# Doubled edge steps with the first scatter in front, an expert table by partition, and empty rows from two queues

## The reference, cut to what matters

```
xn  = layernorm(x)
# graph layer, twice: mean over incoming edges, two products
agg = segment_sum(xn[src], dst) / max(degree, 1)
h   = tanh(agg @ W1_l.T + xn @ W1_r.T + b1)
out = segment_mean(h[src], dst) @ W2_l.T + h @ W2_r.T + b2
# linear attention over all nodes with feature map elu(t @ P) + 1
mix = (q_phi @ (k_phi.T @ v)) / (q_phi . sum(k_phi)) @ w_proj + b_proj
x   = x + out + mix
# mixture of 8 experts, one per node (top 1)
xf  = layernorm(x); e = argmax(xf @ Wr + br)
x   = x + relu(xf @ W1[e] + b1[e]) @ W2[e] + b2[e]
```

## Time and profile before

| | |
|---|---|
| median of 3 runs | 2527.06 us (2523.83 to 2531.4) |
| profiled execution | 2525.53 us, its span 2523.7 us |
| granted TensorE clock, mean | 0.977 |
| TensorE busy | 2369.1 us (94%) |
| VectorE / ScalarE / GpSimd busy | 67% / 44% / 47% |

### The profile page before, as it was taken

How to read it: one execution, slowest core, us unless ns; L and a number is a source line. 1 busy time by engine, 2 the same in 40 slices (tenths; PEclk the granted TensorE clock), 3 DMA queues, 4 the chain that set the end, 5 groups by cost and what they waited for, 6 DMA issues and landing times.

```text
span 2523.7 us, 37527 instructions
## 1 busy us (share of the span) xinstructions
PE 2369.1 (94%) x11497; PEld 1899.4 (75%) x11497; DVE 1702.6 (67%) x3521; ACT 1110.4 (44%) x2047; POOL 1186.2 (47%) x1087
## 2 busy tenths in 40 slices
PE   5999999999999999899999988888999997886997
PEld 4788888888888887788888866666777776664896
DVE  5577777777787774343443437878888775995676
ACT  3454554444444443343443333323332332664775
POOL 5676776666666664000000004655555551774444
PEclk8999999999999999899999999999999999998999
DMA  9866755555555554454444436787888777995885
GB/s 373 277 172 175 204 140 154 156 125 132 159 126 129 157 131 127 175 213 188 186 164 184 192 138 199 207 215 209 239 232 231 222 216 262 358 367 206 253 259 189
DMA packets 159280, 507.40 MB, mean 201 GB/s; under 512 B 30274, under 2 KB 30786, under 8 KB 127026
## 3 DMA queue, kind: packets, MB, share of 16 engines
q1 hardware_dynamic: 109956, 377.52, 41.8%
q0 software_dynamic: 49200, 128.35, 23.1%
HBM read 263.83 MB, written 241.96 MB: 200 GB/s over the span
## 4 chain that ended last, share of the span: by engine, by line
PE 84%; DMA 7%; DVE 3%; ACT 2%; issue 2%; SPq 1%; POOL 1%; POOLq 0%; DVEq 0%; ACTq 0%
PE bank L1347 56%; PE bank L1398 8%; PE bank L1354 6%; DMA agg_d<-O,eidx 5%; PE bank L1531 3%; PE bank L1603 3%; PE bank L1462 2%; PE bank L439 1%; PE bank L440 1%; ACT r_xn L960 1%; PE bank L1593 1%; PE bank L1595 1%; DMA a_x<-in_x 1%; DVE pd L1174 1%; PE bank L1473 1%
## 5 line engine op out<-in xcount | busy, mean ns | idle before, releaser
L400 POOL DMA_INDIRECT agg_d<-O,eidx x160 | 274.4, 1715 | 216.9 <-DMA agg_d<-O,eidx 156.6
L336 POOL TENSOR_TENSOR G_low<-G,G_high 128x512 fp32r<-128x512 f32 x160 | 237.3, 1483 | 226.7 <-ACT G_high L461 226.6
L383 POOL DMA_INDIRECT G<-y_d,esrc x80 | 87.3, 1091 | 528.7 <-DMA y_d<-b_y 516.3
L419 DVE SCALAR_TENSOR_TENSOR Sj<-erow,dstf,tri 128x128 f32<-128x128 int32 x160 | 190.8, 1193 | 26.1 <-DMA agg_d<-O,eidx 26.0
L461 ACT CAST G_high<-G 128x512 fp32r<-128x512 f32 x160 | 99.2, 620 | 198.1 <-DVE G L1059 175.8
L428 DVE SCALAR_TENSOR_TENSOR eidx<-cnt,todump,dstf 128x1 int32<-128x1 f32 x160 | 157.7, 986 | 7.6
L930 ACT CAST qz_high<-low 128x512 fp32r<-128x512 f32 x80 | 49.7, 621 | 231.6 <-PE bank L1347 153.7
L758 POOL TENSOR_TENSOR pd<-pd,low 128x512 f32<-128x512 f32 (+1 forms) x80 | 143.0, 1788 | 0.0
L336 POOL TENSOR_TENSOR a_xn_rows_low<-a_x,a_xn_rows_high 128x512 fp32r<-128x512 f32 x80 | 142.6, 1782 | 0.2 <-ACT a_xn_rows_high L828 0.2
L802 POOL DMA_INDIRECT out<-x_out,x_id x87 | 83.4, 959 | 115.6 <-DVE x_out L1309 113.4
L1347 PE MATMUL bank<-Wk_high,xnT_high 128*128 128x512 f32 x320 | 127.8, 400 | 6.3 <-DVE xnT_low L336 6.3
(11 more groups left out here) (221 smaller groups left out, 7308.7 us busy)
## 6 DMA issues: line engine op xcount, KB each, us to landing
x_rows<-xs_d SPq DMA_DIRECT2D x87, 260.0 KB, 3.1
agg_d<-zero SPq DMA_DIRECT2D x20, 1040.0 KB, 20.0
b_agg<-agg_d SPq DMA_DIRECT2D x20, 1040.0 KB, 8.8
a_x<-in_x SPq DMA_DIRECT2D x20, 1024.0 KB, 6.5
agg_d<-z_halves SPq DMA_DIRECT2D x20, 1024.0 KB, 5.9
q_d<-q_rows SPq DMA_DIRECT2D x80, 256.0 KB, 2.4
r_d<-r_rows SPq DMA_DIRECT2D x80, 256.0 KB, 3.7
r_in<-r_d SPq DMA_DIRECT2D x20, 1024.0 KB, 6.8
```

What stands on the lines that cost most here:

```text
L336: return eng.tensor_tensor(out_, full, high.bitcast(F32), ALU.subtract)
L383: pool.indirect_dma_start(G[:, j, :], None, table, bass.IndirectOffsetOnAxis(ap=esrc[:, b, j:j + 1], axis=0)).then_inc(e_g[j], 16)
L400: pool.indirect_dma_start(agg, bass.IndirectOffsetOnAxis(ap=eidx[:, j, 0:1], axis=0), O[:, j, 0:width], None, compute_op=ALU.add).then_inc ...
L419: dve.scalar_tensor_tensor(Sj[:, :], row, dstf[:, b, j:j + 1], tri[:, :], ALU.is_equal, ALU.mult, accum_out=cnt[:, j:j + 1]).then_inc(e_cn ...
```

## The change

GpSimd's order in doubled steps, before L, G, S, L, G, S, becomes S, L, G, L, G, S. Single steps are as before.

```
-                for te in edge_steps(turn, k):
+                edges = edge_steps(turn, k)
+                for te in edges[0:len(edges) - 1]:
+                    edge_scatter(pool, 1, *te, agg2_d.ap(), D)
+                for te in edges:
                     edge_low(pool, 1, *te)
                     edge_gather(pool, 1, *te, y_d.ap())
+                for te in edges[-1:]:
                     edge_scatter(pool, 1, *te, agg2_d.ap(), D)
```

```
-            for e in range(EXP):
+            for e in range(0, EXP, 2):          # SyncE
...
+            act.wait_ge(r_tb, 1)                # ScalarE
+            act.wait_ge(r_pad, 16)
+            for e in range(1, EXP, 2):
+                end = act.value_load(runi[0:1, e:e + 1], min_val=0, max_val=EXP * REG - P)
+                act.dma_start(xs_d[bass.ds(end, P), :], pad[:, :]).then_inc(r_pad, 16)
```

```
-            made(13, dve.tensor_tensor(past[one, :, :], order[one, None, :].to_broadcast(wide), ..., ALU.is_ge))
-            made(14, dve.tensor_tensor(gone[one, :, :], past[one, :, :], ..., ALU.mult))
-            made(15, dve.tensor_reduce(tabf[one, 0, :], past..., op=ALU.add))
-            made(16, dve.tensor_reduce(tabf[one, 1, :], gone..., op=ALU.add))
-            made(17, dve.scalar_tensor_tensor(tabf[one, 1, :], order[one, :], float(P), tabf[one, 1, :], ...))
-            made(18, dve.tensor_copy(tabE[one, :], tabf[one, 0, :]))
-            made(19, dve.tensor_scalar(tabS[one, :], tabf[one, 1, :], run[one, EXP - 1:EXP], None, ALU.min))
+            made(12, dve.scalar_tensor_tensor(gone[:, :], until[:, most], lane, jump[:, most], ALU.is_le, ALU.mult,
+                                              accum_out=tabf[:, 1:2]))
+            made(13, dve.tensor_scalar(past[:, :], until[:, most], lane, 0.0, ALU.is_le, ALU.add,
+                                       accum_out=tabf[:, 0:1]))
+            made(14, dve.scalar_tensor_tensor(tabf[:, 1:2], lane, float(P), tabf[:, 1:2], ALU.mult, ALU.add))
+            made(15, dve.tensor_tensor(tabf[:, 1:2], tabf[:, 1:2], run[:, EXP - 1:EXP], ALU.min))
+            dve.wait_ge(r_tb, 16)
+            dve.tensor_copy(tabS[one, :], bank[0][one, P:P + XT]).then_inc(r_tb, 1)
+            dve.tensor_copy(tabE[one, :], bank[0][one, 0:XT]).then_inc(r_tb, 1)
...
+            pe.wait_ge(r_tb, 15)                # TensorE, behind its last routing step
+            for i in range(2):
+                last = pe.transpose(bank[0][0:1, i * P:(i + 1) * P], tabf[:, i:i + 1], ident[:, :])
+            last.then_inc(r_tb, 1)
```

More of the change, by code:

```diff
@@ L28 @@
 CW = 1120
-TB = 19
+TB = 18
 ALU = mybir.AluOpType
@@ L192, in build @@
         b1s = word("b1_rows", 312, [EXP, EH])
-        brc, rev, first = word("br", 288, [1]), cst[:, 296:304], cst[:, 304:312]
+        brc, lane, rev, first = word("br", 288, [1]), cst[:, 290:291], cst[:, 296:304], cst[:, 304:312]
         order, idn = cst[:, 824:824 + XT], cst[:, 1040:1040 + NT]
@@ L205, in build @@
         xh = word("x_relu", 1536, [2, 2, P], F32R)
-        past, gone = at("x_past", 13, shape=[P, EXP - 1, XT]), at("x_gone", 13.3125, shape=[P, EXP - 1, XT])
-        tabf = at("x_table_f", 13.625, shape=[P, 2, XT])
+        past, gone = at("x_past", 13, shape=[P, EXP - 1]), at("x_gone", 13.3125, shape=[P, EXP - 1])
+        tabf = at("x_table_f", 13.625, shape=[P, 2])
         tabE, tabS = (at(f"x_table{i}", 13.75 + 0.0625 * i, dt=I32, shape=[P, XT]) for i in range(2))
@@ L1266, in made @@
                 dve.wait_ge(r_tb, n)
-            one = slice(0, 1)
+            one, most = slice(0, 1), slice(0, EXP - 1)
             dve.wait_ge(r_ch, CH * NG)
             made(1, dve.tensor_copy(runi[one, :], run[one, :]))
-            made(2, dve.scalar_tensor_tensor(cn[one, :], run[one, :], P - 1.0, first[one, :], ALU.add, ALU.subtract))
-            made(3, dve.tensor_scalar(nt[one, :], cn[one, :], 7, None, ALU.arith_shift_right))
-            made(4, dve.tensor_copy(ntf[one, :], nt[one, :]))
@@ L1274, in _ @@
-            made(5, dve.tensor_copy(until[one, 0:1], ntf[one, 0:1]))
-            for e in range(1, EXP - 1):
[L1276 to L1286, removed]
@@ L1287, in _ @@
-            made(17, dve.scalar_tensor_tensor(tabf[one, 1, :], order[one, :], float(P), tabf[one, 1, :],
-                                              ALU.mult, ALU.add))
-            made(18, dve.tensor_copy(tabE[one, :], tabf[one, 0, :]))
+            made(2, dve.scalar_tensor_tensor(cn[:, :], run[:, :], P - 1.0, first, ALU.add, ALU.subtract))
+            made(3, dve.tensor_scalar(nt[:, :], cn[:, :], 7, None, ALU.arith_shift_right))
+            made(4, dve.tensor_copy(ntf[:, :], nt[:, :]))
@@ new lines, in _ @@
+            dve.tensor_scalar(jump[:, :], ntf[:, :], -float(P), float(REG), ALU.mult, ALU.add)
+            made(5, dve.tensor_copy(until[:, 0:1], ntf[:, 0:1]))
+            for e in range(1, EXP - 1):
+                made(5 + e, dve.tensor_tensor(until[:, e:e + 1], until[:, e - 1:e], ntf[:, e:e + 1], ALU.add))
+            made(12, dve.scalar_tensor_tensor(gone[:, :], until[:, most], lane, jump[:, most], ALU.is_le, ALU.mult,
+                                              accum_out=tabf[:, 1:2]))
@@ L1293, in _ @@
+            dve.tensor_copy(tabS[one, :], bank[0][one, P:P + XT]).then_inc(r_tb, 1)
+            dve.tensor_copy(tabE[one, :], bank[0][one, 0:XT]).then_inc(r_tb, 1)
+            dve.wait_ge(r_tb, TB)
             expert_of = {}
@@ L1640 @@
     consts[:, P:2 * P] = 1.0
+    consts[:, 290] = p
     consts[:, 296:304] = EXP - np.arange(EXP)
```

## The result

| | before | after |
|---|---|---|
| median | 2527.46 us (2523.08 to 2533.4, 13 runs) | 2533.63 us (2531.1 to 2539.68, 13 runs) |
| ratio to before, 95% | | 1.0026 [1.0018, 1.0035] |
| profiled execution | 2525.53 us | 2538.71 us |

The change costs 6.6 us (4.5 to 8.8), 0.26%: slower beyond the spread of the runs. The median stays under the 0.3% (7.6 us) at which the prediction let slower begin, and the interval reaches past it. The forecast was 2536, the range 2521 to 2542. The profiled execution of after lies 5 us above its own median, so its trace shows somewhat more than the medians do.

The account below looks back on a forecast made before the run. TensorE was taken to bound the kernel (84% of the chain), stalling in doubled steps on the edge scatter's DMA. Order +12.9, table 0 and queues -3.5 gave +9.4: 2534.9 us on the profiled execution, 2536 on the median; range 2521 to 2542.

Parts of the forecast that it names:

- S0 held by the landing, no earlier for standing in front: Doubled steps: the first scatter already waits for the previous scatter's landing, so putting it first sends it out no earlier.
- step 10: S0, S1: Step 10, no scatter in flight: first scatter at 1539.1 not 1542.49, second at 1547.4 not 1550.29; scatters 2.9 us early.
- opening sum after S0: TensorE's edge sum opening the step after a doubled one starts 6.5 us after the first scatter instead of 3.04.
- part 1: GpSimd's new order inside the six doubled steps of the mixing stage: +12.9 us.
- the clock: Step 22's doubled gap drops TensorE's granted clock for part of its product: +1.5 us, within the order's +12.9.
- part 2: Expert table before the expert stage: two transposes and copies replace four results over 87 columns; no cost or gain.
- part 3: Eight empty rows issued from two queues before the expert stage, so the first load comes earlier: -3.5 us.
- The same recursion: Step-by-step sum of TensorE and scatter delays over doubled steps 10 to 30, ending at 11.4 us.
- That delays add: Mixing stage: TensorE's delay in each doubled step stays and carries on, reaching 11.4 us after step 30.
- Rival 1: Delays do not add, only the scatters carry on: 7.5 us, with 3.5 off +4, 2531 us; chance 0.2.
- Rival 2: Landings before each first scatter shorten to 4.8 us, so the order gives about -1: 2522.5 us; chance 0.2.
- Rival 3: The two queues bring nothing, as ScalarE's issues are slow or transfers stretch: 2539.5 us; chance 0.1.

Follow-up runs that it names:

- e1: The kernel before with only GpSimd's new order in doubled steps, table and empty rows unchanged: 2534.8 us, 1.0028 of before.
- e4: The full change with GpSimd's old order kept, so only the new table and the two queues against before: 2528.3 us, 1.0004.
- e6: The kernel before with the first gather of a doubled step moved behind its first scatter: 2529.0 us, 1.0005 of before.
- e3: The kernel before with both low halves and both gathers ahead of both scatters in doubled steps: 2528.21 us, 1.0000 of before.
- e5: The kernel before with the first scatter between second low half and its gather in doubled steps (first of all in step 10): 2522.99 us, 0.9978.
- e12: The same kernel as e5, measured a second time against before: 2524.95 us, 0.9987.
- e11: e7 with a second empty tile behind each first, sixteen in all: 18.10 us from first table result to first load, one run.
- e7: The kernel before with the eight empty tiles from two queues and the old table: 12.70 us from first table result to first load, 13.36 before.

## Why the prediction was right, and where its sum was not

| step | predicted | measured |
|---|---|---|
| S0 held by the landing, no earlier for standing in front | as before | intervals before S0 in the five steps 46.6 us in after, 41.4 in e1, 38.9 in before, 38.0 to 41.4 over the old order |
| step 10: S0, S1 | 1539.1, 1547.4 | 1539.42, 1548.48 |
| opening sum after S0 | 6.5 us (+3.4) | 5.75 (+2.7) |
| S1 after S0 | 7.9 us | 7.07 |
| part 1 | +12.9, of it +1.5 the clock | +7.1 (4.6 to 9.6); in the traces about half of it the clock |
| part 2, the table | 0 | 0 (12.67 against 12.70 us) |
| part 3, the queues | -3.5 | -0.7 in the trace; +1.0 (-1.5 to +3.5) in e4, with the table |
| sum | +9.4 | +6.6 (4.5 to 8.8) |

**The mechanism** holds: the scatter doesn't go out earlier for standing in front, and what TensorE waits for has moved behind it. One of the five was misread: in step 18 of before S0 waits for ScalarE's copy (1.73 us), which ends 1.1 us behind the landing (1605.95 + 5.19 = 1611.14), so 5.2 and not 6.6 is that landing; standing in front doesn't help there either. **The range and the direction** hold too, but in part by luck, through terms whose errors offset each other: part 1 was some 6 us too high and part 3 some 3 us or more too favourable. Of its two neighbouring outcomes the prediction gave slower than 0.3% the larger chance, 0.45, and the one that came, within 0.3%, 0.42.

**The low half's length.** The sum took 1.85 us for both L's. The first took 1.80 us and the second 1.28. That is 0.57 of the 0.78 between 6.52 and 5.74; a gather slot of 1.31 us where 1.45 was taken is 0.14 more. Between 7.97 and 7.07 the same short L stands with 0.56, two such slots with 0.28.

The prediction put the short L down to an idle VectorE, and that reading is wrong. VectorE in before beside the L of 1603.21 (1.29 us), and in after beside the two L's of 1579.86 (1.80 us) and 1583.13 (1.28 us):

```profile
1603.36 0.69 DVE L1151 TENSOR_TENSOR low<-phi_q,bank 128x512 f32<-128x512 f32 x1
1603.96 0.70 DVE L419 SCALAR_TENSOR_TENSOR Sj<-erow,dstf,tri 128x128 f32<-128x128 int32 x1
```

```profile
1579.76 2.45 DVE L336 TENSOR_TENSOR qz_low<-low,qz_high 128x512 fp32r<-128x512 f32 x1
...
1582.74 0.67 DVE L1161 TENSOR_TENSOR low<-phi_q,bank 128x512 f32<-128x512 f32 x1
1583.70 0.88 DVE L419 SCALAR_TENSOR_TENSOR Sj<-erow,dstf,tri 128x128 f32<-128x128 int32 x1 [0.28 <-DMA agg_d<-O,eidx]
```

VectorE works beside the short L's too, on a subtraction with one operand in `bank` (TensorE's output memory) and on the selection matrix. Beside the long L it works on a subtraction whose operands are both tiles of the on-chip memory that GpSimd uses, and that one is stretched as well: 2.45 us, where the same shape takes 0.68 at 1582.14. So an L's length, 1.28 or 1.80 us, goes with what VectorE is doing and not with whether it does anything. A few long L's (1.88 us at 1660.65 in after) stand beside no VectorE row at all, and those stay unexplained. The Trainium skill ("GPSIMD Engine Reference", Specifications) names contention with VectorE instructions that have two on-chip inputs. The row of 2.45 us agrees with it. The selection matrix's instruction also has its inputs on-chip, and the L's of 1.29 and 1.28 us beside it stayed short, so the rule alone doesn't foretell each row.

The same recursion with +2.7 and +1.4 gives -0.2, 2.5, 5.2, 6.6 and 8.0 us after steps 14 to 30. Step 10's head start was 1.8 us at S1 and not 2.9, as the landing behind S0 took 8.3 us where 7.0 was taken (and 1539.1 + 7.0 + 0.8 is 1546.9, not the 1547.4 of the prediction); with that the last value is 9.1.

**That delays add** is the step that failed most, as far as the runs tell. The recursion with the measured lengths gives 9.1 us of idle time; the traces show 5.5 (31.0 against 25.5). With the growth of TensorE's busy time in the table of orders, 5.1, it would be 14 in the profiled executions, which show 10.5. Rival 1, in which only the scatters carry on, gives with the measured lengths -1.8 (step 10), +1.3, -0.35 and twice +1.45, then +2.7 at the last opening sum: 4.75. e6 moved the sum almost alone, by 1.3 to 1.5 us in each of five steps, for +1.2, and e3 took some 2.5 us a step out of it, with S0 itself later, for nothing. All this lies nearer to rival 1. Its whole time, 2531 with the 3.5 off, was as near to 2533.63 as the forecast's 2536, and its 7.5 for part 1 is nearer to e1's 7.1 than 12.9 is, though it has no term for the clock. How far the delays add can't be settled closer: the idle time is a mean over two and four executions whose own spread is 3.5 and 5.3 us.

**The clock** was put at +1.5 for one step. In the table of orders TensorE's busy time grows by 5.1 us, about as much as its idle time. Of the five groups each of the four kernels with the old order has one at a granted clock of 1.00 with TensorE busy for 29.1 to 29.3 us (in before the group of 1623.36, in the other three the one ahead of it). In after and e1 no group is above 0.95, and the last stands at 0.84 and 0.88, where it was 0.91 to 0.95. Together with the idle time that is 10.5 us in the profiled executions, which in after and e1 lie 5 us above their medians; e1's medians give 7.1. The halves of that 7.1 are therefore an estimate from two traces.

**Rival 2** is out: the intervals before S0 didn't shrink, though S0 stood ready at once: its landings took 5.7 to 10.3 us in after, not 4.8. **Rival 3** is what part 3 did. The sum moved the last landing by the four issues saved and counted the landings at before's lengths; they grew by 2.0 to 2.5 us in the median, and the last scatter's by 1.8. It had the rule beside it: the Trainium skill ("DMA: Bandwidth & Descriptors", Issuing engines are not separate DMA queues) says a second issuer saves the issue time alone. Even that bound was generous, as 4 x 1.31 us of issues became 0.7 us of time. The estimate by bytes took the page's fastest slice, 373 GB/s; the hole of after ran at 272.

## What to carry to other kernels

On an in-order queue, put behind a waiting instruction only what nobody else waits for; here that meant both low halves ahead of the scatter and the second gather behind it, which neither of the two kernels had (e5 and e12, 0.22 and 0.13% faster than before). Before a chain is reordered, write down for each element whether its own input would be ready at the new place: a scatter held by a landing gains nothing from going first, and a low half held by ScalarE gives its delay to all behind it. A saved issue counts as saved time only if the landings it overlaps keep their length.

## What the runs showed of the hardware that was not expected

- Four issues of 260 KB DMAs on each of two queues at once run 1.6 and 1.5 us apart (5.24 and 4.91 us in all), against 1.31 on one queue alone, and land in 4.4 and 4.9 us against 2.4. In e11, with eight on each queue, they run 1.3 us apart on either, so two queues don't always slow each other's issues.
- In after a gap of 2.30 us left the matmuls behind it at 0.40 us, and behind a second of 1.81 us, 0.9 us of matmuls later, they took 0.63 us for the next 3.4 us. Whether the second gap had a part isn't told: in before, step 19, a single gap of 2.04 us was followed by the same fall some 1.4 us after it, and in step 23 a gap of 2.34 us by none (group of 1623.36 at 1.00). In the same place as the 2.04 us gap e4 and e7 have 1.29 and 0.89, and no fall.
- The five groups of the mixing stage, with the order unchanged, differ by 5.9 us from one profiled execution to another (177.7 to 183.6), nearly as much as the whole effect of the change: what a change is worth there takes medians, and one trace shows only the mechanism.
